# A planned single-core kernel: new durations for its planner, late key powers, and weights made ternary by ScalarE's Sign instead of VectorE's clip

## What is computed

```python
x = x + tanh(g_xattn[0]) * mamba(ctx, z=layernorm(x))        # selective scan: 512 channels, 16 states
x = x + tanh(g_ffn[0])   * bit_ffn(layernorm(x))             # ternary weights, 512 -> 2048 -> 512
x = x + tanh(g_xattn[1]) * attention(layernorm(x), ctx)      # 16 heads of 128, q and k normalised
x = x + tanh(g_ffn[1])   * experts(layernorm(x))             # 4 experts by token position

# in bit_ffn, for each of gate_w, val_w, out_w (each 2048 x 512):
gamma_w = clip(mean(abs(w)), 1e-5)
w_dq    = clip(round(w / gamma_w), -1, 1) * gamma_w          # -1, 0 or 1 times gamma_w
```

## Time and profile before

| | |
|---|---|
| median of 3 runs | 1849.45 us |
| the profiled execution | 1849.74 us |
| its span, first to last instruction | 1847.9 us |
| TensorE busy in it | 1755.0 us (95%) |
| VectorE busy | 1301.5 us (70%) |
| ScalarE busy | 963.8 us (52%) |
| GpSimd busy | 681.7 us (37%) |
| mean granted TensorE clock | 0.988 |
| DMA | 292.11 MB, 158 GB/s over the span |

### The profile page before, as it was taken

One profiled execution on the slowest core, in us unless ns is written; L12 is line 12 of the kernel. 1 busy time (PEld: TensorE's weight loads), 2 busy tenths in 40 slices (PEclk: granted clock), 3 DMA queues, 4 the chain that ended last, 5 costly groups with the idle time before them and its releaser, 6 DMA issues.

```text
span 1847.9 us, 19510 instructions
## 1 busy us (share of the span) xinstructions
PE 1755.0 (95%) x6114; PEld 805.4 (44%) x6114; DVE 1301.5 (70%) x1899; ACT 963.8 (52%) x1919; POOL 681.7 (37%) x696
## 2 busy tenths in 40 slices
PE   8999899869998998999999999999999899999999
PEld 4333344324443444444444444444444344445543
DVE  4989786989999699899889898877532444412221
ACT  7989876447555546557466557554444334320100
POOL 2434422356463246457214456642123333300000
PEclk9999999989999999999999999999999999999999
DMA  7999823678851138887115779621122899837110
GB/s 262 244 293 291 259 100 109 188 186 198 207 145 37 52 82 210 222 208 196 57 36 114 178 188 249 159 58 57 46 69 80 235 285 292 237 100 273 40 51 28
DMA packets 159045, 292.11 MB, mean 158 GB/s; under 512 B 18424, under 2 KB 51704, under 8 KB 156000
## 3 DMA queue, kind: packets, MB, share of 16 engines
q1 hardware_dynamic: 141664, 227.95, 39.3%
q0 software_dynamic: 17280, 62.92, 17.6%
HBM read 169.51 MB, written 58.26 MB: 123 GB/s over the span
## 4 chain that ended last, share of the span: by engine, by line
PE 67%; DVE 15%; issue 6%; ACT 5%; DMA 5%; POOL 2%; SPq 1%; DVEq 0%; ACTq 0%; POOLq 0%
PE p L837 10%; PE p L814 8%; PE p L797 8%; PE p L848 7%; PE p L884 6%; PE p L692 5%; DVE s_M L1016 5%; PE p L771 4%; PE p L820 3%; PE p L899 3%; PE p L776 3%; PE p L741 2%; DVE s_M L1011 2%; DVE s_M L1023 2%; DVE s_U L1165 1%
## 5 line engine op out<-in xcount | busy, mean ns | idle before, releaser
L1016 DVE TENSOR_TENSOR_SCAN s_M<-s_M 128x1024 f32<-128x1024 f32 x128 | 297.3, 2323 | 12.5 <-ACT s_M L1277 10.0
L1165 DVE CUSTOM_DVE_ANT_0 s_U<-p,s_U 128x512 f32<-128x512 f32 x256 | 187.7, 745 | 167.0 <-PE p L814 164.7
L814 PE MATMUL p<-s_U 128*128 128x512 f32 x512 | 266.8, 609 | 4.5 <-DVE s_U L1165 3.4
L797 PE MATMUL p<-s_U 128*128 128x512 f32 x512 | 253.6, 604 | 5.1 <-DMA s_U<-in_Wq 2.4
L1517 POOL DMA_DIRECT2D s_u<-s_M x120 | 112.8, 941 | 358.1 <-DVE s_M L1023 323.7
L1558 POOL TENSOR_SCALAR s_U<-s_U 128x512 f32<-128x512 f32 x256 | 237.7, 947 | 6.4
L848 PE MATMUL p<-s_U 128*128 128x512 f32 x512 | 223.7, 592 | 0.0
L837 PE MATMUL p<-s_U 128*128 128x512 f32 x472 | 215.0, 596 | 2.7 <-ACT s_U L1414 2.5
L1414 ACT COPY s_U<-p 128x512 f32<-128x512 f32 x196 | 105.5, 593 | 171.1 <-PE p L820 169.7
L1277 ACT ACTIVATE s_M<-s_dl,s_small 128x511 f32<-128x511 f32 x256 | 170.3, 717 | 45.5 <-DVE s_M L1016 41.8
L1409 ACT ACTIVATE s_U<-s_U 128x512 f32<-128x512 f32 x256 | 181.6, 710 | 5.3
(11 more groups left out here) (194 smaller groups left out, 2469.5 us busy)
## 6 DMA issues: line engine op xcount, KB each, us to landing
s_u<-s_M POOLq DMA_DIRECT2D x120, 512.0 KB, 7.5
s_bc<-bc_scratch SPq DMA_DIRECT2D x96, 256.0 KB, 4.6
k_scratch<-s_U SPq DMA_DIRECT2D x16, 1024.0 KB, 9.0
v_scratch<-s_U SPq DMA_DIRECT2D x16, 1024.0 KB, 6.1
s_U<-in_Wq SPq DMA_DIRECT2D x64, 256.0 KB, 6.6
s_U<-k_scratch SPq DMA_DIRECT2D x64, 256.0 KB, 5.4
s_U<-rk_scratch SPq DMA_DIRECT2D x64, 256.0 KB, 4.8
s_U<-in_Wo SPq DMA_DIRECT2D x64, 256.0 KB, 4.3
```

The costliest lines, as they stand in the source:

```text
L797: ins = e.matmul(banks[bk][:], wqq[j % 2][:, k, :], axT[b % 2][:, k, :], start=(k == 0), stop=(k == 3))
L814: e.matmul(banks[bk][:], qT[j % 3][:, k * 128:(k + 1) * 128], kT[j % 2], start=True, stop=True).then_inc(S["a_s"], 1)
L1016: e.tensor_tensor_scan(w, dA[i % 2], w, 0.0, ALU.mult, ALU.add).then_inc(S["m_s"], 1)
L1165: e.tensor_tensor_reduce(out=Pm[j % 2][:, k, :], in0=banks[ABANK[kind, j, k]][:], in1=rkb[j % 2], scale=rq[:, k:k + 1], scalar=-3.0e38, op ...
```

## The change

Five things are changed.

1. The durations in the planner's six tables are written anew (nearly all become a little shorter, `nq` on TensorE longer), and a step now begins 0.25 us behind what it needs instead of 0.15 us.
2. The last two key powers (q == 3 and b > 1) need `xst` 3 of batch 0 in the plan, so that GpSimd has them behind the last inverse root of that layernorm. The first `s` of the attention no longer needs the last step of K in the plan, only the last `v`.
3. `clip` is gone from Q, on VectorE and in the plan; `put` needs `rnd` alone.
4. `put` is ScalarE's Sign with a bias of -12582912 held in a tile of one column (`down`), in place of Copy with that bias as a number. A rounded weight of at least 12582912 + 1 becomes 1, one of at most 12582912 - 1 becomes -1, and 12582912 itself 0: what clip and subtraction made.
5. GpSimd writes `down` at the end of its setup, and the first `put` waits for that.

```diff
-        QUANT += [("clip", w, c)] if c < 4 else []
...
-            part((kind, i), [("DVE", 1.25)] + ([("POOL", 0.8), ("SUM", 5.0)] if i < 2 * NS - 2 else []))
+            part((kind, i), [("DVE", 1.14)] + ([("POOL", 0.8), ("SUM", 5.0)] if i < 2 * NS - 2 else []))
...
-        elif kind == "clip":
-            out.append(("Q", [("DVE", 1.3)], [(0, "rnd", w, c)], (0, kind, w, c), [], []))
         elif kind == "put":
-            out.append(("Q", [("ACT", 2.0)], [(0, "clip", w, c)], (0, kind, w, c), [], []))
+            out.append(("Q", [("ACT", 1.82)], [(0, "rnd", w, c)], (0, kind, w, c), [], []))
...
-        needs = {... "pw": [("K", at.get((b, q, "r", 0))), ("K", n - 1)], ...
+        needs = {... "pw": [("K", at.get((b, q, "r", 0))), ("K", n - 1)] + [(0, "xst", 3)] * (q == 3 and b > 1), ...
...
-        needs = {... "s": [(NB, "nt", j, 0)] + ([] if j else [("K", len(KV) - 1)]) + ...
+        needs = {... "s": [(NB, "nt", j, 0)] + ([] if j else [("K", KV.index((NB - 1, 3, "v", 3)))]) + ...
...
-                ready = ended[s, i, k - 1] + 0.15
+                ready = ended[s, i, k - 1] + 0.25
...
+        down = sb("down", [128, 1])
...
-                    elif kind == "clip":
-                        e.wait_ge(S["q_rnd"], 4 * w + c + 1)
-                        e.tensor_scalar(stg[c], stg[c], MAGIC - 1.0, MAGIC + 1.0, ALU.max, ALU.min).then_inc(S["q_cut"], 1)
...
-                        e.wait_ge(S["q_cut"], i + 1)
-                        e.activation(dst, stg[c], ACT.Copy, bias=-MAGIC, saturate=False).then_inc(S["q_put"], 1)
+                        e.wait_ge(S["q_rnd"], i + 1)
+                        if i == 0:
+                            e.wait_ge(S["p_set"], 12)
+                        e.activation(dst, stg[c], ACT.Sign, bias=down[:], saturate=False).then_inc(S["q_put"], 1)
...
+                e.memset(down[:], -MAGIC).then_inc(S["p_set"], 1)
```

60 lines of the change are left out of this document (30 added, 30 removed).

## The result

The changed kernel takes 1896.34 us, the median of 4 runs (1889.88 to 1902.87); the kernel before took 1850.35 beside it (4 runs). The ratio is 1.0249, with a 95% interval of 1.0208 to 1.0290: slower by 46 us, where 15 us less were forecast. The profiled execution took 1897.09 us, its span 1895.3 us.

The account below looks back on a forecast made before the run. TensorE was taken as the bound, so only its idle or lower-clock time could go, chiefly at the handoff to attention: -12.9 + 1.9 - 2.8 - 3.0 + 1.5 = -15.3 us, giving 1834 us, range 1825 to 1847.

Parts of the forecast that it names:

- Term 1: Handoff from keys to attention: TensorE's fourth xxt transpose moves from 374.93 to 362.0, -12.9 us (bounds -13.6 and -9.8).
- Term 2: Before the first query: a new TensorE wait for the query weights of 1.1 to 2.6 us, taken as +1.9.
- Term 3: First two queries and transposes: no lower clock after the long wait, -2.8 us (bound about -1.1).
- Term 4: First heads: VectorE reaches the first score near 376.0 and the later bubble shrinks, -3.0 us (bounds -4.4 and 0).
- Term 5: Key phase: earlier weight loads on full DMA queues delay it, +1.5 us (bounds -4 and +8.4).
- The rest of the order: From 411 us on: TensorE's idle time may fall or grow, no reason for a sign, 0 (bounds -6 and +8).
- Sign: ScalarE's puts: Sign in place of Copy adds at most 1 us to an engine that is not late, counted 0.
- A: Rival: the DMA queues take the gain in the key phase, 1842 to 1846 us, chance 0.20.
- B: Rival: FFN rows of batches 2 and 3 come too early for VectorE, TensorE waits at yt, 1866 us, chance 0.07.
- C: Rival: the order of the later stages gains 6 us too, 1827 us, chance 0.10.
- D: Rival: Sign needs its own table, up to 24 loads on ScalarE, about 1850 us; chance 0.03 together with the unknown.
- The bounds named for being wrong: TensorE idle above 25 us in the first 350, or idle from 411 us differing from 29.5 + 14.0 by over 6.

Follow-up runs that it names:

- e10: The changed kernel with the old durations for attention's steps and the second and third thresholds behind 17 and 31 scans: 1868.58 us (1.0085).
- e5: The changed kernel with the second and third thresholds planned later, behind 17 and 31 scans: 1870.61 us, median of four runs, one of them 1892.98.
- e13: The same program as e5, run again: 1866.29 us (1861.55 to 1868.78).
- e6: The changed kernel with GpSimd rescaling only 16 of 512 columns of each probability tile, leaving out most of the normalisation: 1863.66 us (1.0056).
- e1: The kernel before in its own order, with the clips issuing nothing and the put done by Sign: 1861.06 us (1.0034).
- e15: The changed kernel with old attention durations, the old latency of 0.15 us and the thresholds later: 1868.39 us (1.0078).

## Why the prediction was wrong

TensorE of the changed kernel at the handoff, in order of time, answers to the earlier trace rows.

```profile
381.05 1.47 PE L747 MATMUL p<-s_identf,s_U 128*128 128x128 f32 x12
382.36 1.88 PE L774 MATMUL p<-s_U 128*128 128x512 f32 x4
384.17 1.06 PE L780 MATMUL p<-s_U,s_ones 128*32 128x512 f32 x8
385.17 3.70 PE L774 MATMUL p<-s_U 128*128 128x512 f32 x8
388.71 0.60 PE L747 MATMUL p<-s_identf,s_U 128*128 128x128 f32 x4
392.32 3.67 PE L795 MATMUL p<-s_U 128*128 128x512 f32 x8 [3.02 <-DMA s_U<-in_Wq]
...
402.28 1.02 PE L812 MATMUL p<-s_U 128*128 128x512 f32 x2
...
410.37 1.49 PE L795 MATMUL p<-s_U 128*128 128x512 f32 x2 [4.08 <-DMA s_U<-in_Wq]
```

And two stretches of the changed kernel, columns as in the earlier trace rows:

```profile
150.00:200.00 50.00, 31.75 (x81) 12.63 (x80) 27.30 (x21) 28.14 (x43) 17.50 (x9) 0.80 0.84 236
412.00:414.00 2.00, 2.00 (x3) 0.68 (x2) 2.00 (x1) 0.00 (x0) 0.00 (x0) 0.50 1.08 197
```

- **Term 1 (handoff, -12.9 us): the mechanism right, the size too large.** The wait of 11.86 us is gone, and the transpose has none. But it stands at 388.71, which less the 17.2 us of the key phase is 371.5 and not 362.0. The gap is filled with key rows: the 6.3 us that I counted, and some 5 us more that had fallen behind, since TensorE had done 5.2 us less by the first mark (270.2 us busy in 310, before 275.4 in 293). That is work moved, not gained. With the long stop cured it is hardly better: in e10, whose first mark is 1.4 us late, the transpose stands at 372.16, 370.8 without these, against 374.93 before.
- **Term 2 (a new wait for the query weights, 1.1 to 2.6, taken as 1.9): right in place, 3.02 us.** A second one of 4.08 us, for the third query's weights, was not seen. SyncE issued that load at 398.81 behind a key power's store, and it took 11.4 us to land among the loads of keys and values, where the median of before was 5.2.
- **Term 3 (clock, -2.8): right at its place, given back in part later.** The first query's eight products take 3.67 us, before 5.67, so 2.0 and not 2.2 us; they are one head's query and not two. The granted clock is 1.00, that is 2.4 GHz, from 375 to 410 us, also behind the wait of 3.02 us. The dip that I had priced at 1.7 us came behind the second wait, of 4.08 us: 0.50 from 412 to 414 us, that is 1.2 GHz.
- **Term 4 (first heads, -3.0): wrong.** The first score began at 403.5 on VectorE, 386.3 without the key phase's 17.2, against 376 in the forecast, and from there to head 4 it took 63.7 us where it took 52.8. The second wait for query weights lies there (4.08 us), and the first two slow scans (447.59 and 462.8).
- **Term 5 (DMA in the key phase, +1.5, bounds -4 and +8.4): the step that failed first.** It measured +17.2, one to 3 of them perhaps chance. I had treated the transfers as what could wait and priced them by the queues' shares. The queues were not what made the long stop: from 150 to 200 us the changed kernel moved 236 GB/s, less than the 297 of before. It was the orders of the engines, each waiting for the next, and e5 undid it with one line. Only the smaller wait at 103 us (7.86 for 5.07) had a load that landed late. What stands behind each waiting instruction was followed for the handoff only, not for the thresholds and the key powers, though the new order moved both.
- **The rest of the order (0, bounds -6 and +8): the step that failed most.** From the first score on 37.0 us were lost (47.4 - 10.4). I saw "no reason for a sign". The reason was to be had from the trace of before: VectorE busy 818.9 of 969 us, and its scans there hardly waited for a decay (10.0 us in 128, most of it ahead of 400 us); e13 against e5, and e6, show what comes when it does. That a stage runs without loss can hang on its exact order: every other order tried here lost 2 to 45 us between head 0 and head 48, and none gained. So a new order had to be priced as a risk of one sign.
- **Sign (0): near enough**, 2.01 to 2.20 us in place of 1.92, some 2 us in all. The clips that went were worth nothing (e1), where term 1 counted on them for 4.6 us at least.
- **Rivals.** A (queues) had the place right and the mechanism wrong. B (FFN rows of batches 2 and 3 too early) did not happen: at `yt` (L679) TensorE waits 1.77 us twice. C (a later gain) had the sign wrong. D (Sign's own table) did not happen: no table load stands between 35 and 239 us, and all twelve Signs do. The bounds named for being wrong, 25 us of idle time and a change of over 6 us from 411 on, were both broken: 39.8, and 59.6 + 11.3 for 29.5 + 14.0.

What stays open: why the last 15 to 18 us of e10 and e15 are lost; no run tells those small waits apart. Nor does one tell whether the place of the thresholds or that of the key power made the stop in the key phase.

## What to carry to other kernels

Where a planner sets the order, fresh and truer durations are not an improvement to be assumed: the order before lost less behind the first score than all the others tried here, and a new one must be timed part by part. Before pricing a new order, follow each engine's instruction that waits for another (a threshold, a store behind a power, a scan behind its decay) through what stands behind it, round all the engines if need be. Test two cures together as well as one by one before adding up what each is worth. When one program's times lie in two groups, set a trace of each side by side before explaining anything by the code.
